# Moving the low parts, the second transpose and one output product in a two-layer attention and feed-forward kernel

## What is computed

```
x = x + attention_0(layernorm(x), ctx)     # 16 heads of 64, 77 keys
x = x + W_down(silu(W_gate n) * (W_up n))  # n = layernorm(x), hidden width 768
x = x + attention_1(layernorm(x), ctx)
x = x + quantised_product(layernorm(x))    # 256 x 256, int8 steps
```

## Time and profile before

| | us |
|---|---|
| median of 3 runs | 1758.61 |
| lowest, highest | 1753.06, 1759.71 |
| profiled execution | 1756.78 |
| its span, first to last instruction | 1754.7 |
| layer 0 bodies with feed-forward | about 282 to 1190 |
| layer 1 bodies | about 1190 to 1720 |

### The profile page before, as it was taken

How to read it: one execution, slowest core, us unless ns; L and a number is a source line. 1 busy time by engine, 2 the same in 40 slices (tenths; PEclk the granted TensorE clock), 3 DMA queues, 4 the chain that set the end, 5 groups by cost and what they waited for, 6 DMA issues and landing times.

```text
span 1754.7 us, 75093 instructions
## 1 busy us (share of the span) xinstructions
PE 1566.0 (89%) x27410; PEld 1358.7 (77%) x27410; DVE 1375.5 (78%) x3522; ACT 1324.4 (75%) x5514; POOL 1245.7 (71%) x1966
## 2 busy tenths in 40 slices
PE   7999778898888888898888888889999999999995
PEld 4556568787888878888888787777888888888884
DVE  6777557777777777777777777678999999999996
ACT  6665767777777677777777776677888888888883
POOL 5110467777777777777777777567999999999984
PEclk9999989999999899999999999999999999999998
DMA  9997796866666676666766787767989989888995
GB/s 251 342 321 259 168 191 136 153 148 146 152 149 149 140 155 156 144 146 144 162 141 152 144 156 135 140 133 153 196 198 194 193 198 193 197 191 198 191 185 115
DMA packets 740023, 307.79 MB, mean 175 GB/s; under 512 B 629201, under 2 KB 725361, under 8 KB 737841
## 3 DMA queue, kind: packets, MB, share of 16 engines
q1 hardware_dynamic: 738049, 299.32, 77.1%
q0 software_dynamic: 1840, 6.82, 1.4%
HBM read 87.09 MB, written 65.54 MB: 87 GB/s over the span
## 4 chain that ended last, share of the span: by engine, by line
PE 36%; POOL 18%; DVE 18%; issue 10%; DMA 5%; SPq 2%; DVEq 0%; ACT 0%; POOLq 0%
PE psum L333 26%; POOL pr L1707 6%; PE psum L1274 5%; PE psum L1237 4%; POOL hT_l L1698 4%; POOL p L1720 4%; DMA x2T<-x 3%; POOL p L1712 3%; DVE nmax L1544 2%; DVE oT_l L362 2%; DVE x L373 2%; POOL rs L395 2%; SPq L1125 1%; DVE st L378 1%; DVE sg L1509 1%
## 5 line engine op out<-in xcount | busy, mean ns | idle before, releaser
L1421 ACT ACTIVATE ex<-psum,nmax 128x77 f32<-128x77 f32 x2048 | 635.7, 331 | 66.5 <-DVE nmax L1544 51.4
L1707 POOL TENSOR_TENSOR pr<-ex,rden 128x308 f32<-128x308 f32 x512 | 399.3, 780 | 186.1 <-DVE rden L1549 185.7
L1421 ACT ACTIVATION_READ_ACCUMULATOR ex<-psum,nmax 128x1 f32 x2048 | 435.7, 213 | 0.0
L1712 POOL TENSOR_TENSOR p<-pr,p 128x308 f16<-128x308 f32 x512 | 388.3, 758 | 40.8
L333 PE MATMUL psum<-xT,wq_h 128*64 128x256 f16 x4064 | 356.3, 277 | 0.9 <-DMA xT<-x 0.9
L1544 DVE TENSOR_REDUCE nmax<-psum 128x4 f32<-128x308 f32 x512 | 238.0, 465 | 68.8 <-PE psum L1237 68.5
L333 PE MATMUL psum<-xT,wq_l 128*64 128x256 f16 x2032 | 282.4, 274 | 0.0
L333 PE MATMUL psum<-wo_h,oT_h 128*64 128x256 f16 x1792 | 259.0, 284 | 14.1 <-DVE oT_l L362 13.7
L333 PE MATMUL psum<-wo_h,oT_l 128*64 128x256 f16 x1792 | 257.3, 282 | 0.0
L333 PE MATMUL psum<-wo_l,oT_h 128*64 128x256 f16 x1792 | 256.5, 281 | 0.0
L1720 POOL CAST p<-pr 128x308 f16<-128x308 f32 x509 | 227.4, 447 | 38.9 <-DMA pT<-p 6.2
(11 more groups left out here) (173 smaller groups left out, 3504.7 us busy)
## 6 DMA issues: line engine op xcount, KB each, us to landing
keys<-ks SPq DMA_DIRECT2D x16, 1232.0 KB, 7.7
kb<-keys SPq DMA_DIRECT2D x256, 77.0 KB, 2.7
vb<-vals SPq DMA_DIRECT2D x128, 154.0 KB
vals<-vs SPq DMA_DIRECT2D x64, 256.0 KB, 4.5
x_pair<-in_x_dram SPq DMA_DIRECT2D x32, 256.0 KB, 3.0
pT<-p SPq DMA_TRANSPOSE x512, 3.2
x_res<-in_x_dram SPq DMA_DIRECT2D x32, 256.0 KB, 3.1
mid_x<-y SPq DMA_DIRECT2D x32, 256.0 KB, 2.4
```

The lines of the kernel that those rows point to most:

```text
L1421: last = act.activation(ex[i][:, t, b, :], SC[:, t, b * NK:(b + 1) * NK], ACT.Exp, bias=nmax[i][:, t, b:b + 1], accum_out=den[i][:, t, b:b ...
L1707: pool.tensor_tensor(pr[:, t, :, :], ex[i][:, t, :, :], r, ALU.mult).then_inc(s_p, 1)
L1712: pool.tensor_tensor(d[:, t, 1, :, 0:NK], pr[:, t, :, :], d[:, t, 0, :, 0:NK], ALU.subtract).then_inc(s_pl, 1)
```

## The change

- POOL: the low parts of chunks 2, 3 and 5 are made one probability half earlier than before (chunk 2 still in part 0, chunk 5 in part 1), and `rs2` ahead of the first half of unit 0.
- DVE: `x2` is made ahead of `sg` and `hf` of chunk 4, where it stood behind them and behind `qT_l`.
- ACT: `x216`'s high part moves from the end of part 1 to part 2, behind `oT_h` and `qT_h`; the high part of chunk 5 moves behind `oT_h`.
- SP: the transpose `x2T` is issued ahead of both transposes of probabilities of part 2.
- PE: `down(0)` moves behind `project` of part 2. Its waits are split: the low parts of chunks 0 to 3 at its start, that of chunk 4 before that chunk, that of chunk 5 before the last.

Nothing is added or taken away, and layer 1's bodies keep their order. The diff, cut to its core (each hunk is in the body of the engine named above it):

```diff
# SP
+                        if u == 2 and lay[-2] == 0:
+                            turn_second_rows(h - 2)
                         if turning:
                             turn_probabilities(n + u - 1, (u - 1) % UNITS, 0)
...
                         if turning:
                             turn_probabilities(n + u - 1, (u - 1) % UNITS, 1)
-                        if u == 2 and lay[-2] == 0:
-                            turn_second_rows(h - 2)
# PE
-                def down(t, o):
+                def down(t, o, b):
                     terms = [(c, hh) for c in range(HC) for hh in (hT_h, hT_l)]
                     for q, (c, hh) in enumerate(terms):
+                        if t == 0 and q == 0:
+                            pe.wait_ge(s_hlp, len(LOW_POOL) * b + LOW_POOL.index(3) + 1)
+                            pe.wait_ge(s_hld, len(LOW_DVE) * b + LOW_DVE.index(1) + 1)
+                        if t == 0 and (c, q % 2) == (4, 0):
+                            pe.wait_ge(s_hld, len(LOW_DVE) * (b + 1))
+                        if t == 0 and (c, q % 2) == (5, 0):
+                            pe.wait_ge(s_hlp, len(LOW_POOL) * (b + 1))
...
-                        if u == 2 and lay[-3] == 0:
-                            pe.wait_ge(s_hlp, len(LOW_POOL) * (h - 2))
-                            pe.wait_ge(s_hld, len(LOW_DVE) * (h - 2))
-                            down(0, bank("down", 0))
...
                             project(n + u - 4, u, four)
                         if u == 2 and lay[-3] == 0:
-                            down(1, bank("down", 1))
+                            down(0, bank("down", 0), h - 3)
+                        if u == 2 and lay[-3] == 0:
+                            down(1, bank("down", 1), h - 3)
# ACT
-                        if u == 2 and lay[-3] == 0:
-                            high_hidden(5, h - 3)
...
+                        if u == 2 and lay[-3] == 0:
+                            high_hidden(5, h - 3)
                         if lay[(u + 1) // UNITS] is not None:
...
                             high(act, qT_h[(u + 1) % 2][:, :, :], RG[(u + 1) % 2], Q_DOWN).then_inc(s_qh, 1)
+                        if u == 2 and lay[-2] == 0:
+                            act.wait_ge(s_x2, QT * (h - 1))
+                            after(act, s_x2d, 16 * (h - 2))
+                            high(act, x216[:, :, 0, :], x2[:, :, :]).then_inc(s_x216h, 1)
...
-                        if u == 1 and lay[-2] == 0:
-                            act.wait_ge(s_x2, QT * (h - 1))
-                            after(act, s_x2d, 16 * (h - 2))
-                            high(act, x216[:, :, 0, :], x2[:, :, :]).then_inc(s_x216h, 1)
# DVE
+                        if u == 1 and lay[-2] == 0:
+                            normalise_rows(dve, 1, x2, x1[1 - odd], mv2, rs2, h - 1, s_x2)
                         if u == 1 and lay[-3] == 0:
                             sigmoid_gate(4, h - 3)
...
-                        if u == 1 and lay[-2] == 0:
-                            normalise_rows(dve, 1, x2, x1[1 - odd], mv2, rs2, h - 1, s_x2)
                         if u == 1 and lay[-3] == 0:
                             sigmoid_gate(5, h - 3)
# POOL
                         if u == 1 and lay[-3] == 0:
-                            low_hidden(2, h - 3)
-                        if u == 2 and lay[-3] == 0:
-                            low_hidden(5, h - 3)
+                            low_hidden(3, h - 3)
...
                             probabilities(h + (u - 1) // UNITS, (u - 1) % UNITS, 1)
                         if u == 1 and lay[-3] == 0:
-                            low_hidden(3, h - 3)
+                            low_hidden(5, h - 3)
+                        if u == 0 and lay[-3] == 0:
+                            low_hidden(2, h - 3)
+                        if u == 0 and (lay[-2] == 0 or lay[-3] == 0):
+                            inverse(pool, 1, ve2, rs2, h - 1)
...
                             probabilities(h, u, 0)
-                        if u == 0 and (lay[-2] == 0 or lay[-3] == 0):
-                            inverse(pool, 1, ve2, rs2, h - 1)
```

## The result

| | before | after |
|---|---|---|
| median, us | 1759.16 (4 runs, 1753.06 to 1766.96) | 1647.48 (4 runs, 1644.60 to 1651.03) |
| ratio, with 95% interval | 1 | 0.9364 [0.9321, 0.9406] |
| profiled execution, its span, us | 1756.78, 1754.7 | 1644.60, 1642.7 |
| mean granted clock of TensorE | 0.968 | 0.995 |
| layer 0 body, mean of 26, us | 28.94 | 26.03 |

The forecast was 1658, with a range of 1634 to 1700; 6.4% were gained where 5.7% were forecast.

What follows compares the result with a forecast made beforehand. Waits between engines, on a chain through POOL's list and x2T, were taken to bound the kernel. 86.8 us from 26 bodies plus 12 from the tail, together 99, took 1756.78 to 1658 us, range 1634 to 1700.

Steps and rivals of the forecast that it cites:

- The chain: Layer 0 before: POOL's low part and probabilities, SP's transposes, x2T, gate_up(0), scores; once a body, 28.94 us.
- the new loop: Layer 0 after: PE scores to value product, ACT oT_h, POOL chunk 5 to nmr1, xn, exponentials; 25.6 us a body.
- nothing is added: ACT and DVE: moved high parts, 0.63 and 0.44 us, only swap places with their neighbours.
- the walked leg over PE and oT_h: Stretch of the loop: PE from unit 0's scores through value product, 10.8 us, then ACT's oT_h and chunk 5's high part, 1.0.
- the sum over the bodies: Layer 0's 26 bodies, each falling from 28.94 to 25.6 us: 86.8 us gained.
- The four tail bodies: End of layer 0, 30.5 us each beside layer 1's start: 2.5 us gained each, the middle of 0 and 5.
- 2.4 GHz throughout: PE's clock: stops of 3.03 us shrink to under 1 us, so no slow stretches and no charge.
- alone it is worth nothing: PE's order: project fills part of the wait for hT_l, but down(0) is beside the chain; gain 0.
- PE alone bounds: Rival: the loop's handoffs overlap better, a body takes 24.4 us, 1624 us in all; chance 0.07.
- POOL and DVE meet: Rival: three more meetings in the new loop, 0.4 to 0.5 us each, bodies of 26.9, 1697 us; chance 0.15.
- x2T no earlier than its data: Rival: x216's low part is late, a body gains only the transpose's issue, 1.28 us; 1722 us; chance 0.05.
- Slower by the clock: Rival: 10.2 us a body at 1.2 GHz on PE's loop work costs 5.1, gives back 3.3; 1803 us; chance 0.04.

Runs made afterwards that it cites:

- e6_no_pe: The changed kernel with PE's part undone, down(0) ahead of project again with whole waits; 1646.89 us.
- e11_e4_pe: The kernel before with POOL's, SP's and PE's parts of the change, ACT and DVE as before; 1636.84 us.
- e4_pool_sp: The kernel before with POOL's and SP's parts of the change, PE, ACT and DVE as before; 1634.27 us.
- e17_kb: The changed kernel with rs1 and nmr1 ahead of unit 1's second half, yn behind part 3's last exponentials, load of keys behind x2T; 1590.76 us.
- e18_kb_x216: e17_kb with ACT's high part of x216 back at the end of part 1; 1593.55 us.
- e5_no_sp: The changed kernel with SP's part undone, x2T behind both transposes of probabilities of part 2 again; 1800.79 us.
- e1_pe: The kernel before with PE's part alone, down(0) behind project of part 2, without the split inside down; 1790.89 us.
- e2_sp: The kernel before with SP's part alone, x2T ahead of both transposes of probabilities of part 2; 1706.13 us.
- e3_pool: The kernel before with POOL's part alone, low parts of chunks 2, 3, 5 and rs2 one probability half earlier; 1770.11 us.
- e13_e4_nm1_yn: e4_pool_sp with rs1 and nmr1 ahead of unit 1's second half on POOL and yn behind the last exponentials on ACT; 1622.34 us.

## Why the prediction came out

**Right: what bounded the kernel.** The chain was the one over x2T and POOL's list. PE's wait for hT_l, the largest on PE's list, was beside it: e6_no_pe and e11_e4_pe put PE's order at zero within the change, while SP's and POOL's parts by themselves give all of the gain, and 13 us more.

**Right: the new loop.** Its order and its lengths hold: 6.37 for 6.5 on POOL, 10.78 for 10.8 on PE, and 25.68 round the loop where the sum gave 25.6 to 26.0 and 25.6 was taken. The 25.58 of e4_pool_sp is not this loop.

**Mis-sized: ACT's and DVE's parts.** The step that failed is "nothing is added", with x2 on DVE put at a delay of 1.1 us and a gain of 1.4, so at nothing. On DVE, x2 in front of chunk 4 takes 1.26 or, stretched beside POOL, 1.77 us, so that hf of chunk 5 comes later than the walked leg over PE and oT_h, by 0.06 or 0.57 us, 0.32 in the mean. That and the 0.08 between 25.6 and 25.68 are nearly the whole 0.43 us by which a body is longer than forecast; 26 x 0.43 = 11 us are what the sum over the bodies lost. Measured against a kernel without them, ACT's and DVE's parts cost 0.40 us a body.

**Left out: start, tail and end.** They brought 36.4 us where 12 were counted. The first body with x2T took 32.98 us before and 24.56 after, 8.4 us, because the kernel before had a stop there and ran slowly behind it. Windows of before:

```profile
256.90:263.70 6.80, 5.39 (x52) 4.61 (x54) 2.84 (x7) 1.90 (x10) 1.89 (x3) 0.50 0.77 169
```

The other 6.2 us of the start were there at the first x2T, and 2.7 of them already at the first exponentials (195.5 and 192.8 us). The place of the first x2T also differs by 10 us between e17_kb and e18_kb_x216 (257.4 and 247.4), so these 6.2 cannot be put down to the change. The four tail bodies gained 4.2 us each, not the 2.5 taken as the middle of 0 and 5; the body behind them, which the forecast's 12 include, lies in the last stretch. The two errors have opposite signs: 11 lost in the loop, 24 gained around it, 13 in all between 99 and 112 us.

**The clock.** "2.4 GHz throughout" came true, and its reason in the main: the stops of 3.03 us are gone and no slow stretch came, though stops of up to 1.84 us stayed, where under 1 was forecast. What was wrong is "alone it is worth nothing" for PE's order: alone it costs 32 us, for it moves the stop onto the chain.

**The rivals.** *PE alone bounds* did not occur (26.03, not 24.4), and in e17_kb it does. *POOL and DVE meet* came in part: pr takes 0.88 and its rounding 0.78 at 607.91 and 608.85, where others take 0.70 and 0.44. The Trainium skill, "GPSIMD Engine Reference", section "Key points", says that POOL shares its SBUF interfaces with VectorE and that there is contention between them; these rows agree with that. They cost nothing against the forecast, since the walk's 6.5 on POOL holds a slow pr too. The meeting that did cost is one that no part of the prediction named, of x2 on DVE with a low part on POOL: half a us in half of the bodies, where the rival had three meetings in each. *x2T no earlier than its data* is excluded: it is issued 0.1 us behind the keys. *Slower by the clock* did not occur in the change; in e5_no_sp, one DMA's place away from it, the mechanism did, with 1800.79. That this is close to the rival's 1803 is chance: the loop without SP's part is longer than the rival had it, and the slow stretches are shorter, 6.2 us a body instead of 10.2.

**What was to show it.** x2T came every 26.03 us, for 25 to 26; PE's wait for hT_l was 0, for under 15; ACT's for nmr1 83.7, for at least 60. POOL's wait for the high part of chunk 5 was 0.36 or 0.99, 0.69 in the mean, for 0.6; with the other chunks it is about 1.6 a body (49.6 in all). Layer 1's part was 589.0 long, for 593.9.

## What to carry to other kernels

A long wait is worth only what the chain says, and before it is moved one must ask what stands behind it: here 3 us of idle time in front of other matmuls made the same program 1.8% slower. Test the parts of an order alone and in pairs, since two waits that end at nearly the same time hide each other: -53 and +11 us apart were -125 together. Where bodies come in two lengths, look for the step whose own duration has two values. After every gain read the chain anew and look also at the engine that only issues: with one transpose moved ahead of two others, and later one load behind it, these reorderings went from 28.9 to 23.9 us a body, where PE is full.

## What the runs showed of the hardware

Between 250 and 1150 us the granted clock of TensorE fell to 0.50 (1.2 GHz) for 3.40 or 6.80 us at a time. The kernel before, e1_pe, e2_sp, e3_pool and e5_no_sp have 111 such stretches. 110 of them began during a stop of PE that lasted 2.7 us or more, or within 1.3 us behind one; the other one came behind a stop of 2.05 us, and e13_e4_nm1_yn's only one behind 1.72. In the change and the other seven kernels, where no stop of PE in these 900 us was over 1.91 us, there was none. But of the stops of 2.7 us or more only some had a stretch: 20 of 29 (before), 25 of 30 (e1_pe) and 8 of 27 (e2_sp). What decides that was not separated. The Trainium skill, "TensorE: Matmul & The Clock Gate", Part 1, says that throttled is the default state and activity releases it; these stretches, which come with idle time, agree. Unexpected was that the price depends on the place: 1.70 us for each 3.40 behind a stop in front of gate_up(0) (e1_pe), nothing for 3.40 behind a stop in front of down(0) (before). A stretch of 6.80 us there did cost: 30.0 for 28.75 us in the kernel before, 30.02 for 27.17 in e2_sp.

Two steps that meet on DVE and POOL did not share the loss: of x2's second half on DVE and a low part on POOL, each over 128x256 elements and 0.09 us apart at their starts, either DVE's took 0.91 us instead of 0.40 or POOL's 0.84 instead of 0.67.
